# Feed forward of a two-expert mixture: all experts for every row, or routed rows gathered in slots

## What is computed

```python
x = x + attention_a(layernorm(x))   # 8 heads of 128, relative positions
x = x + ffn(layernorm(x))
x = x + attention_b(layernorm(x))   # 16 heads of 8, causal, one key head
x = x + ffn(layernorm(x))           # the same weights again

def ffn(x):                         # E = 8 experts, H = 256
    gate_scores = softmax(x @ Wg.T)
    topk_val, topk_idx = top_k(gate_scores, 2)
    topk_val = topk_val / (topk_val.sum(-1) + 1e-9)
    comb = (one_hot(topk_idx, 8) * topk_val[..., None]).sum(-2)
    for e in range(8):
        a, b = split(x @ W1[e].T + b1[e], 2)
        out += ((a * sigmoid(b)) @ Wo.T + bo) * comb[..., e]
```

## Time and profile before

| | us |
|---|---|
| median of 3 runs | 2801.4 |
| the profiled execution | 2800.0 |
| its span in the trace | 2798.3 |
| TensorE busy | 2620.7 (94%) |
| VectorE busy | 2037.5 (73%) |
| ScalarE busy | 1656.8 (59%) |
| GpSimd busy | 385.7 (14%) |
| bytes moved by DMA | 321.63 MB, nearly all in the first attention |

### The profile page before, as it was taken

How to read it: one execution, slowest core, us unless ns; L and a number is a source line. 1 busy time by engine, 2 the same in 40 slices (tenths; PEclk the granted TensorE clock), 3 DMA queues, 4 the chain that set the end, 5 groups by cost and what they waited for, 6 DMA issues and landing times.

```text
span 2798.3 us, 45154 instructions
## 1 busy us (share of the span) xinstructions
PE 2620.7 (94%) x14496; PEld 2042.4 (73%) x14496; DVE 2037.5 (73%) x5225; ACT 1656.8 (59%) x3430; POOL 385.7 (14%) x813
## 2 busy tenths in 40 slices
PE   4999999999999999999999889989998989988998
PEld 3788788888888888888888667755555555545776
DVE  4677766767767777677776678878777777773887
ACT  3566666666666666665666445536666656655454
POOL 1000000000000000000110233402222212222344
PEclk8999999999999999999999989969999999998999
DMA  3665566566665666656666000000000000000000
GB/s 125 226 220 200 181 224 210 192 211 208 210 211 198 210 211 209 209 206 210 226 233 209 10 1 1 1 1 1 1 1 1 1 1 1 1 1 1 9 9 16
DMA packets 97587, 321.63 MB, mean 115 GB/s; under 512 B 11924, under 2 KB 25620, under 8 KB 97140
## 3 DMA queue, kind: packets, MB, share of 16 engines
q1 hardware_dynamic: 92650, 312.84, 32.6%
q0 software_dynamic: 1584, 4.33, 0.5%
q10 hardware_dynamic: 3120, 1.57, 0.2%
HBM read 158.53 MB, written 157.29 MB: 113 GB/s over the span
## 4 chain that ended last, share of the span: by engine, by line
PE 80%; DVE 11%; ACT 5%; issue 3%; POOL 1%; DMA 0%; SPq 0%; DVEq 0%; ACTq 0%; POOLq 0%
PE ps L243 8%; PE ps L245 7%; PE ps L244 7%; PE ps L630 7%; PE ps L743 5%; PE ps L605 5%; PE ps L604 5%; PE ps L781 5%; PE ps L643 4%; PE ps L645 4%; PE ps L644 4%; PE ps L763 4%; PE ps L675 4%; PE ps L676 4%; PE ps L677 4%
## 5 line engine op out<-in xcount | busy, mean ns | idle before, releaser
L910 ACT ACTIVATE a_Ph<-ps 128x512 fp32r<-128x512 f32 x512 | 305.9, 597 | 467.8 <-PE ps L630 467.7
L1215 DVE CUSTOM_DVE_ANT_0 a_sp<-ps,a_sp 128x1024 f32<-128x1024 f32 x256 | 313.2, 1223 | 180.0 <-PE ps L245 175.9
L980 ACT ACTIVATE r_P<-ps 128x512 f32<-128x512 f32 (+3 forms) x768 | 327.9, 491 | 187.1 <-PE ps L763 182.8
L1221 DVE TENSOR_TENSOR a_Pl<-ps,a_Ph 128x512 fp32r<-128x512 f32 x512 | 349.2, 682 | 10.0 <-ACT a_Ph L910 9.8
L604 PE MATMUL ps<-a_fa,a_ua 128*128 128x384 f32 (+2 forms) x960 | 327.2, 353 | 19.3 <-DVE a_fb L1176 13.9
L931 ACT ACTIVATE r_y<-ps 128x256 f32<-128x256 f32 x512 | 194.6, 385 | 216.6 <-PE ps L677 212.4
L903 ACT ACTIVATE a_sp<-a_sp,a_nm 128x1024 f32<-128x1024 f32 x256 | 295.0, 1152 | 32.1 <-DVE a_nm L1215 31.4
L630 PE MATMUL ps<-ident,a_sp 128*128 128x128 f32 x2048 | 309.0, 273 | 0.0
L743 PE MATMUL ps<-r_K,r_Q 128*128 128x512 f32 (+3 forms) x768 | 282.5, 403 | 18.2 <-DVE r_mx L1366 12.8
L630 PEld LDWEIGHTS ps<-ident,a_sp 128*128 128x128 f32 x2048 | 250.8, 141 | 61.7 <-issue 0.6
L605 PE MATMUL ps<-a_fb,a_ub 86*128 86x384 f32 (+2 forms) x960 | 290.8, 318 | 0.0
(11 more groups left out here) (217 smaller groups left out, 5676.0 us busy)
## 6 DMA issues: line engine op xcount, KB each, us to landing
scr<-a_rt SPq DMA_DIRECT2D x256, 576.0 KB, 3.1
a_sp<-scr SPq DMA_DIRECT2D x256, 512.0 KB, 4.4
a_wc<-wsp SPq DMA_DIRECT2D x24, 512.0 KB, 5.5
wsp<-a_wc SPq DMA_DIRECT2D x8, 512.0 KB, 5.6
a_ub<-a_ua SPq DMA_DIRECT2D x64, 44.0 KB
a_w1st<-in_w1t POOLq DMA_DIRECT2D x8, 256.0 KB, 4.6
out<-x SPq DMA_DIRECT2D x4, 512.0 KB, 3.2
a_w1r<-in_w1r POOLq DMA_DIRECT2D x8, 254.0 KB, 4.4
```

Source lines behind the costliest of these rows:

```text
L910: e.activation(self.Ph[:, n % 3, :], ps[:, 4 + n % 2, :], ACT.Copy).then_inc(S["p_hi"], 1)
L980: e.activation(self.P[:, pt, off:512], ps[:, bank, off:512], ACT.Exp).then_inc(S["b_exp"], 1)
L1215: e.tensor_tensor_reduce(out=w, in0=ps[:, 2:4, :].rearrange("p a n -> p (a n)"), in1=w, scale=-1.0, scalar=3e38, op0=ALU.add, op1=ALU.min, ...
L1221: e.tensor_tensor(self.Pl[:, n % 3, :], ps[:, 4 + n % 2, :], self.Ph[:, n % 3, :].bitcast(F32), ALU.subtract).then_inc(S["p_lo"], 1)
```

## The change

The feed forward no longer runs all experts for every row. For each row the two experts are turned into two slots, places in an array of rows sorted by expert, in which each expert's rows begin at a multiple of 128. The arrays lie in DRAM: `xsd` for rows that come in and `gsd` for gated results, one pair for batches 0 to 2 (part 0) and one for batch 3 (part 1). Rounding each expert up to whole tiles gives at most 55 and 23 tiles, and that many are always computed. The units are:

- `m_rank`: nine small matmuls number the rows of each expert; `m_slot`: a chain of VectorE instructions makes slots and the table that says which expert a tile belongs to.
- `m_disp`: VectorE writes a normalized row tile to one of two buffers (`xd`), and GpSimd issues two indirect DMAs that write its 128 rows to their slots. VectorE waits before it until the writes from the same buffer have landed.
- `m_load`, `m_turn`: the queue of SyncE loads four tiles of slots, TensorE transposes them, ScalarE and VectorE split them.
- `m_mm`: TensorE reads the expert of the tile from a table into a register and multiplies with that expert's weights; ScalarE takes the tanh of half of b, VectorE gates. Nothing is weighted or added here. `m_store`: two tiles of results go to `gsd`.
- `m_gath`: GpSimd issues two indirect DMAs that read the two results of each of the 128 rows of a tile, into one of three buffers; `m_sum`: ScalarE and VectorE weight and add them; `m_fin`, `m_proj` as `f_fin`, `f_proj` before. `m_bias` adds the weighted bias to x for a whole batch.

The dispatch of batches 0 to 2 stands in the first attention's last quarter for the first feed forward, and in three groups of batch 3 of the second attention for the second one. Batch 3 is dispatched among part 0's tiles, one row tile behind each of the tiles 18 to 25. All 24 fetches of part 0 are issued behind its last store, those of batch 3 behind the last store of part 1. In the first feed forward, the sums and projections that are left then are interleaved with the opening of the second attention, which also takes in the normalization of batch 0; those of batches 1 to 3 now stand in the second attention one batch ahead (before: only batch 3's). The expert weights are split from step 52 of the first attention on, all in buffers of their own. Three DMAs copy rows of the input into `xsd` at the start, so that slots that no row takes hold finite numbers. The normalized high and low parts are kept for two batches only.

```diff
+
+PARTS = ((0, 1, 2), (3,))
+PT = [2 * L // 128 * len(p) + E - 1 for p in PARTS]
+PG = [(t + 3) // 4 for t in PT]
+PP = [(t + 1) // 2 for t in PT]
...
+
+def place(f, b):
+
+    part = [b in p for p in PARTS].index(True)
+    return [("m_rank", f, b)] + ([("m_slot", f, part)] if b == PARTS[part][-1] else [])
+
+
+def disp(f, part):
+    return [("m_disp", f, n) for b in PARTS[part] for n in range(8 * b, 8 * b + 8)]
 
 
...
     for k in range(E + 1):
-        extra.setdefault(64 * (B - 1) + 20 + 4 * k, []).append(("w1", k))
+        extra.setdefault(52 + 2 * k, []).append(("w1", k))
...
+        for i, it in enumerate(splits(1)(b - 1, 7) + gates(0, b - 1) + place(0, b - 1)):
+            extra.setdefault(64 * b + 6 + i, []).append(it)
+    for b, part in ((3, 0),):
+        for i, it in enumerate(disp(0, part) + [("m_bias", 0, c) for c in PARTS[part]]):
+            extra.setdefault(64 * b + 21 + i, []).append(it)
+    for g in range(2):
+        extra.setdefault(64 * 3 + 52 + g, []).append(("m_load", 0, 0, g))
     for s in range(NTI + 6):
...
+    last = [sum(PT[:part + 1]) - 1 for part in range(len(PARTS))]
+    for part in range(len(PARTS) - 1):
+        side.setdefault(last[part], []).extend(("m_gath", f, n) for b in PARTS[part] for n in range(8 * b, 8 * b + 8))
+    back = [[u for u in (("m_sum", f, n), ("m_fin", f, n - 1, 5 + (n - 1) % 2), ("m_proj", f, n - 2, 7)) if 0 <= u[2] < NT]
+            for n in range(NT + 2)]
+    first, every = last[0] + 9, 2.6
+    p, i, nb = [("m_turn", f, 0, 0, 4), ("m_load", f, 0, 2)], 0, 0
+    for k, (part, g) in enumerate(groups):
+        for t in range(4 * g, min(4 * g + 4, PT[part])):
+            p.append(("m_mm", f, part, t, i % 4))
+            if t % 2 or t == PT[part] - 1:
+                p.append(("m_store", f, part, t // 2))
+            if t % 4 == 1 and k + 1 < len(groups):
+                p.append(("m_turn", f, *groups[k + 1], 4))
+                if k + 3 < len(groups):
+                    p.append(("m_load", f, *groups[k + 3]))
+            p += [u for u in side.pop(i, []) if u]
+            if i >= first + every * nb:
+                p += back[nb]
+                nb += 1
+            i += 1
+    p += [("m_gath", f, n) for n in range(8 * B - 8, 8 * B)]
+    p += [u for its in back[nb:10] for u in its]
+    rest = [u for its in back[max(nb, 10):] for u in its]
+    if f == 0:
+        rest.append(("b_zero", 1))
+    return p + (spread(more, rest) if more else rest)
...
-    out = first(0) + prepare(0) + chain(0)
-    late, tail = splits(2)(B - 1, 7) + [("xb_bias", b) for b in range(B)], []
+    opening = splits(2)(0, 7) + first(0) + prepare(0) + chain(0)
+    out, late, tail = [], [("xb_bias", 0)], []
+    rows = disp(1, 0)
+    rows_at = {(3, 1): rows[0:8], (3, 2): rows[8:16], (3, 3): rows[16:24]}
     for n in range(16):
         b, g = n // 4, n % 4
...
+        for i, it in enumerate(rows_at.get((b, g), [])):
+            k = main.index(("b_s", b, g, 1, 3 - i // 2, 2 * (i % 2))) + 1
+            main.insert(k, it)
+            price.insert(k, 0)
...
+        self.xd = sb("xd", [128, 2, 128])
...
+        self.xsd = [nc.dram_tensor(f"xsd{i}", (PT[i] * 128, 128), F32, kind="Internal").ap() for i in range(len(PARTS))]
...
+                self.sig.append(buf("sig", [128, 4, FH]))
+                self.gb.append(buf("gb", [128, 3, 2, FH]))
+                self.acc.append(buf("acc", [128, 2, FH]))
...
+                elif u[0] == "m_store":
+                    _, f, part, n = u
+                    i, k = at(PP, f, part) + n, min(2, PT[part] - 2 * n)
+                    e.wait_ge(S["m_gate"], at(PT, f, part) + 2 * n + k)
+                    if f and part == 0 and n == 0:
+                        e.wait_ge(S["m_sum"], NT)
+                    rows = self.gsd[part][256 * n:256 * n + 128 * k, :].rearrange("(k p) d -> p k d", p=128)
+                    e.dma_start(rows, self.gg[f][:, i % 4, 0:k, :]).then_inc(self.d_gs[i % 4], 16)
 
...
+        i, k = at(PG, f, part) + g, min(4, PT[part] - 4 * g)
+        if g == 0:
+            for s in range(2):
+                e.wait_ge(self.d_scat[s], 16 * (NT * f + 8 * PARTS[part][-1] + 8))
+        if i >= 2:
+            e.wait_ge(S["m_tr"], i - 1)
+        rows = self.xsd[part][512 * g:512 * g + 128 * k, :].rearrange("(k p) d -> p k d", p=128)
+        e.dma_start(self.sx[:, i % 2, 0:k, :], rows).then_inc(self.d_xs[i % 2], 16)
 
     def first_attention_done(self, e):
...
+        if u[0] == "m_disp":
+            _, f, n = u
+            i, part = NT * f + n, [n // 8 in p for p in PARTS].index(True)
+            e.wait_ge(S["m_xd"], i + 1)
+            if i == 0:
+                e.wait_ge(S["d_zero"], 64)
+            if f and n == 8 * PARTS[part][0]:
+                e.wait_ge(S["m_tr"], at(PG, 0, part + 1))
+            for k in range(2):
+                e.indirect_dma_start(self.xsd[part], bass.IndirectOffsetOnAxis(self.slot[:, k, n:n + 1], 0),
+                                     self.xd[:, i % 2, :], None).then_inc(self.d_scat[i % 2], 16)
+        elif u[0] == "m_gath":
+            _, f, n = u
+            i, part = NT * f + n, [n // 8 in p for p in PARTS].index(True)
+            if n == 8 * PARTS[part][0]:
+                end = at(PP, f, part + 1)
+                for p in range(end - 4, end):
+                    e.wait_ge(self.d_gs[p % 4], 16 * (p // 4 + 1))
+            if i >= 3:
+                e.wait_ge(S["m_sum"], i - 2)
+            for k in range(2):
+                e.indirect_dma_start(self.gb[f][:, i % 3, k, :], None, self.gsd[part],
+                                     bass.IndirectOffsetOnAxis(self.slot[:, k, n:n + 1], 0)).then_inc(self.d_gath[i % 3], 16)
 
 
...
+        elif u[0] == "m_mm":
+            _, f, part, t, bank = u
+            i, s = at(PT, f, part) + t, (at(PG, f, part) + t // 4) % 2
+            if t == 0:
+                e.wait_ge(S["m_map"], len(PARTS) * f + part + 1)
+                e.wait_ge(S["w1_lo"], E)
+            if t % 8 == 0:
+                n = min(8, PT[part] - t)
+                e.load(self.expert[t % 16:t % 16 + n], self.mapi[0:1, part, t:t + n])
+            if t % 4 == 0:
+                e.wait_ge(S["m_xlo"], at(PG, f, part) + t // 4 + 1)
+            e.wait_ge(*free[bank])
+            k, cs, hb = e.snap(self.expert[t % 16], min_val=0, max_val=E - 1), slice(128 * (t % 4), 128 * (t % 4) + 128), ps[:, bank, :]
+            wh, wl = (w[:, bass.ds(k, 1), :].rearrange("p k n -> p (k n)") for w in (self.Wh, self.Wl))
+            e.matmul(hb, self.sxh[:, s, cs], wh, start=True, stop=False)
+            e.matmul(hb, self.sxh[:, s, cs], wl, start=False, stop=False)
+            e.matmul(hb, self.sxl[:, s, cs], wh, start=False, stop=True).then_inc(S["m_mm"], 1)
+            free[bank] = S["m_gate"], i + 1
...
+        elif u[0] == "m_mm":
+            _, f, part, t, bank = u
+            i = at(PT, f, part) + t
+            e.wait_ge(S["m_mm"], i + 1)
+            if i >= 4:
+                e.wait_ge(S["m_gate"], i - 3)
+            e.activation(self.sig[f][:, i % 4, :], ps[:, bank, FH:512], ACT.Tanh, scale=0.5).then_inc(S["m_sig"], 1)
+        elif u[0] == "m_sum":
+            _, f, n = u
+            i = NT * f + n
+            e.wait_ge(self.d_gath[i % 3], 32 * (i // 3 + 1))
+            if i >= 2:
+                e.wait_ge(S["m_ftr"], i - 1)
+            e.activation(self.acc[f][:, i % 2, :], self.gb[f][:, i % 3, 0, :], ACT.Copy,
+                         scale=self.pw[:, n, 0:1]).then_inc(S["m_wsum"], 1)
...
+        elif u[0] == "m_disp":
+            _, f, n = u
+            i, b = NT * f + n, n // 8
+            if i >= 2:
+                e.wait_ge(self.d_scat[i % 2], 32 * (i // 2))
+            e.tensor_scalar(self.xd[:, i % 2, 0:127], x[:, n, 0:127], self.mv[:, 1 + b, n % 8, 0:1], self.rs[:, 1 + b, n % 8:n % 8 + 1],
+                            ALU.subtract, ALU.mult).then_inc(S["m_xd"], 1)
...
+        elif u[0] == "m_bias":
+            _, f, b = u
+            if f == 0 and b == 0:
+                e.wait_ge(S["d_zero"], 64)
+            e.wait_ge(S["m_xd"], NT * f + 8 * b + 8)
+            for n in range(8 * b, 8 * b + 8):
+                i = e.scalar_tensor_tensor(x[:, n, :], self.fbo[:, :], self.csum[:, n:n + 1], x[:, n, :], ALU.mult, ALU.add)
+            self.step(i)
...
+        elif u[0] == "m_mm":
+            _, f, part, t, bank = u
+            i, p = at(PT, f, part) + t, at(PP, f, part) + t // 2
+            e.wait_ge(S["m_sig"], i + 1)
+            if t % 2 == 0 and p >= 4:
+                e.wait_ge(self.d_gs[p % 4], 16 * (p // 4))
+
+            e.scalar_tensor_tensor(self.gg[f][:, p % 4, t % 2, :], self.sig[f][:, i % 4, :], 1.0, ps[:, bank, 0:FH], ALU.add,
+                                   ALU.mult).then_inc(S["m_gate"], 1)
+        elif u[0] == "m_sum":
+            _, f, n = u
+            i = NT * f + n
+            e.wait_ge(S["m_wsum"], i + 1)
+            acc = self.acc[f][:, i % 2, :]
```

(1 more changed line is left out.)

700 lines of the change are left out of this document (379 added, 321 removed).

## The result

The changed kernel takes 2769.8 us, median of 5 runs (2762.0 to 2781.2), against 2801.4 us before (5 runs, 2796.0 to 2804.8): ratio 0.9896, 95% interval 0.9866 to 0.9927. It is faster by 31.6 us, 1.0%, where 118 were forecast; the interval is clear of 1. The profiled execution was the fastest of the five, 2762.0 us with a span of 2760.1.

What follows compares the result with a forecast made beforehand. TensorE was taken to bound the first attention, and TensorE's matmuls plus stalls on VectorE and GpSimd the feed forwards. Terms 16 - 114 + 32 - 52 = -118 us gave 2682 profiled, 2683 median; range 2600 to 2790.

Steps and rivals of the forecast that it cites:

- the initialisation: In the first attention, filling the slot arrays with 5.1 MB was to cost 2 us (0 to 12).
- Price of an indirect DMA, 1.1 us: Each indirect DMA of dispatch and fetch was to occupy GpSimd for 1.1 us, between 0.51 and 2.6.
- Landing 4.5 us: Indirect DMAs of dispatch and fetch were to land 4.5 us after issue, lower end 3.2.
- Dispatch, 3.0 us a tile: With two buffers, VectorE's wait for landed writes was to set 3.0 us a row tile, against 2.2 of GpSimd.
- Fetch, 2.2 us a tile: With three buffers, GpSimd's two issues were to set 2.2 us a tile, 70 us for 32 in the second feed forward.
- First attention, +16: The first attention was to grow by 16 us (8 to 35) through ranks, slots, dispatch, bias and initialisation.
- First feed forward, -114: First feed forward and the second attention's opening were to shrink from 316.2 to 202 us.
- 26 tiles of sum, split and projection, 29: Behind the first feed forward's last expert tile, 26 remaining tiles at VectorE's 1.1 us each were to take 29 us.
- Second attention, +32: The second attention was to grow by 32 us (10 to 60): normalizations moved in, ranks, slots and dispatches.
- Dispatch in batch 3, 10: In the second attention's batch 3, three groups with 8 dispatches each were to cost 10 us, partly in idle time.
- GpSimd slower because VectorE holds it up: One reason given for a rival with 1.5 to 1.9 us per indirect issue; that rival's chance 0.17.
- GpSimd slower: Rival: indirect issues take GpSimd 1.5 to 1.9 us, lengthening fetches and dispatches; 2733 us at 1.7; chance 0.17.

Runs made afterwards that it cites:

- e2: Changed kernel with six fetch buffers in place of three: 2730.2 us.
- e9: The changed kernel again, nothing edited, in another group on another chip: 2729.9 us, beside 2797.6 for the kernel before.
- e5: The changed kernel run again, nothing edited, as a control: 2767.1 us, beside 2803.8 for the kernel before.
- e16: The changed kernel again, nothing edited, as control in another group: 2730.5 us.
- e18: The changed kernel again, nothing edited, as control in the last group: 2768.0 us.
- e11: Changed kernel without routing, plain GpSimd DMAs of the same bytes in place of the indirect ones: 2688.8 us, beside 2729.9 unedited (e9).
- e17: The same edit as e11, plain GpSimd DMAs in place of indirect ones, in another group: 2689.7 us, beside 2768.0 unedited (e18).
- e14: Changed kernel without the normalizations of batches 1 and 2 for the second attention, output not valid: 2722.2 us, beside 2730.5 unedited (e16).
- e3: Changed kernel with five dispatch buffers in place of two: 2711.2 us, beside 2802.3 for the kernel before.

## Why the prediction was right or wrong

The direction was right, the size was not: 31.6 of 118 us. Two kinds of step failed. The prediction let the indirect DMAs cost GpSimd's time and the waits that follow from issue and landing, and nothing else; the runs show holds of the three other engines with them, some 38 of the missing 86 us (the difference of the two levels). And terms of the sum were too small: at the lower level, without holds, the gain is 68 to 72 us, and the other 46 to 50 lie above all in the initialisation, in the stretch behind the last tile of the first feed forward, and in the dispatches of batch 3. One by one:

- *Price of an indirect DMA, 1.1 us.* 1.27 from start to start (0.96 of issue and 0.30 between two); the bounds held it. *Landing 4.5 us*: wrong. At the lower level the fetches of the last stage land 2.8 us after issue (2.7 to 4.5), and the dispatches' buffers come free 2.3 to 3.3 us after the second write's issue. The Trainium skill (DMA: Bandwidth & Descriptors, Anatomy of one DMA) gives the estimate of 2.15 for 64 KB that was set aside. These rows lie above it but nearer to it than to 4.5, and the 4.5 us of the earlier trace rows were measured beside 207 GB/s of other traffic.
- *Dispatch, 3.0 us a tile*: 2.6 (8 tiles in 20.8 us), near, but for another reason: GpSimd's 2.54 sets it, with 0.30 us between nearly all its issues, not the landing.
- *Fetch, 2.2 us a tile*: 2.55 at the lower level (80.5 us), 3.01 in the profiled run (94.9). This is the failed term of the second feed forward, +11 and +25 of its 70. It was made up for in part (at the lower level wholly) by part 0, which with the stores landed ended after 92 and not 107. e2 gained nothing by more buffers, at the lower level, where GpSimd waits only 3.3 us for sums in this stage (e9): GpSimd is the bound there. At the upper level more buffers were not run alone.
- *First attention, +16*: +28.5 in the profiled run, and +32 to +36 in the four others of this kernel (e5, e9, e16, e18), at the edge of the 35 that was to be a sign of being wrong. The failed term is the initialisation, 2 with an upper end of 12: from the 64th to the 68th addition of a softmax row the distance to before grew by 11.6 us. The ranks, slots and dispatch, 11: near 15, 5 in each of the three gate stretches; each rank runs its 9 matmuls as 18 passes, 2.2 us at the high clock. The bias, 3: 2.6.
- *First feed forward, -114*: -89. Part 0 ended sooner than forecast, after 85 us and not 94. The 23 tiles of batch 3 were forecast at 23 and took 33, and the stretch behind them 109 where 85 were forecast. Both stretches in the profiled run, then in e9, and the second one in e11 with plain DMAs (columns as in the earlier trace rows):

```profile
1679.20:1712.00 32.80, 26.49 (x124) 20.42 (x125) 16.94 (x43) 14.37 (x38) 16.29 (x17) 0.90 0.63 191
1712.00:1820.90 108.90, 82.27 (x346) 64.96 (x345) 71.26 (x223) 38.87 (x81) 46.68 (x49) 0.65 0.20 60
```

```profile
1682.20:1705.80 23.60, 23.16 (x124) 18.04 (x123) 16.73 (x42) 14.76 (x38) 15.03 (x16) 1.00 0.80 241
1705.80:1815.20 109.40, 81.37 (x347) 63.82 (x344) 71.54 (x225) 39.26 (x81) 47.98 (x50) 0.67 0.22 65
```

```profile
1697.20:1805.40 108.20, 85.65 (x346) 69.15 (x344) 71.62 (x225) 38.63 (x81) 26.93 (x49) 0.60 0.21 63
```

  The 10 us too many among the 23 tiles belong to the upper level: they took 28 to 33 us there (e18, e5, the profiled run) and 24 to 25 at the lower one (e9, e16). The stretch behind is nearly the same at both levels and with plain DMAs (107 in e17), so neither holds nor fetches make it; here the failed term is "26 tiles of sum, split and projection, 29", priced by VectorE. Where the granted clock was 0.50, TensorE was the bound for a while; the profiled run from 1713 us:

```profile
1713.38 0.68 PE L752 MATMUL ps<-ident,m_acc 128*128 128x128 f32 x2
1714.13 0.45 PE L765 MATMUL ps<-woh,m_th 128*128 128x128 f32 x1
...
1715.44 0.65 PE L752 MATMUL ps<-ident,m_acc 128*128 128x128 f32 x2
1716.19 0.45 PE L765 MATMUL ps<-woh,m_th 128*128 128x128 f32 x1
```

  2.06 us a tile, which would be 54 for 26. The granted clock was 0.92 from 1681 to 1710 us, among the tiles, 0.50 from 1710 to 1760 and 0.69 to 0.82 after that, so the price lay between 29 and 54. But TensorE is busy for only 82 of the 109 us and VectorE for 71, and 7.8 us of TensorE's waits are for the opening's normalization (6.3 the longest). How much of the 24 us is the clock, and how much waits between the two, no run separates.
- *Second attention, +32*: +55, or +41 at the lower level. The normalizations' half price held (e14: 10 for two). *Dispatch in batch 3, 10*, failed: each group's eight take 20 us of GpSimd, and from its first group's normalizing step to its last this batch became 37 us longer (22 in e9), against 11 each in batches 1 and 2. In e11, with half the issue time, the attention is 10 us shorter.
- *Its end, unchanged at 13.5*: 21.4. The eight writes of the last group were still being issued at 2543, with VectorE standing before its last passes. e3's buffers took 5 us of it.
- *GpSimd slower because VectorE holds it up*: not at the size that the rival had. The fetch issues of the profiled run take 951 to 1258 ns around a median of 957. Six of the 128 take over 1000 ns, and each of these begins while VectorE is in a pass that reads two operands in SBUF (L1409, the second half of a sum, or L1578). One of them, with the VectorE pass:

```profile
1782.73 0.75 DVE L1578 SCALAR_TENSOR_TENSOR r_Q<-r_yh,lowmask,r_y 128x512 fp32r<-128x512 f32 x1
...
1783.05 1.26 POOL L661 DMA_INDIRECT m_gb<-gsd,m_slot  x1 [0.30 <-issue]
```

  By the Trainium skill (SBUF — State Buffer, SBUF: two separate sides) a VectorE instruction with two SBUF inputs and a GpSimd operation that reads SBUF shut each other out of a shared pair of ports. The trace agrees, but the six together lose 1.0 us. The slowing that mattered is of the other engines, and no rival had it.

The rival "GpSimd slower" gave 2733, close to the 2730 of the lower level, but by luck: it puts 41 us more into the last stage (0.6 times 68, though a stage has 64 fetches), and that stage took 186.3 us there, 2 less than the forecast's.

## What to carry to other kernels

An operation that the trace has never shown deserves a run by itself before a plan is built on it: its issue price was within 16%, but what came with it on the other engines was nearly half of the error. Price the tail of a stage also at the lower clock (0.50 here, 1.2 GHz), by the engine that is then the slowest: a tile was priced at 1.1 us and took 2.06 where TensorE was at that clock. And time an unedited control beside every group of edits: four edits looked like 40 to 59 us each, and were 0 to 19.
